# A written-out timetable of five engines is replaced by another one

## What is computed

```python
x = x + _L0_attn_a_ref(_layernorm(x, axis=-1), Wq, Wk, Wv, Wo)      # 16 heads of 8; causal, window of 32 plus every 64th key
x = x + _L0_ffn_ref(_layernorm(x, axis=-1), k0, k1, k2, s0, s1, s2)  # weights of +1 and -1, 256 -> 512 -> 512 -> 128
x = x + _L0_attn_b_ref(_layernorm(x, axis=-1), ln_g, ln_b, W_in, conv_w, ..., res_scale)   # a selective state space block
x = x + _L0_ffn_ref(_layernorm(x, axis=-1), k0, k1, k2, s0, s1, s2)
```

## Time and profile before

| what | before |
|---|---|
| median of 3 runs | 831.79 us (829.81 to 833.49) |
| span of the profiled execution | 829.0 us |
| lowest run | 829.81 us |
| instructions | 21435 |
| busy: TensorE, VectorE, GpSimd, ScalarE | 94%, 84%, 80%, 72% |
| mean granted TensorE clock | 0.994 |
| moved by DMA | 154.86 MB, 187 GB/s over the span |

### The profile page before, as it was taken

The page is one execution under the profiler, slowest core; times in us unless marked ns, Lnnn a source line. Parts: engine busy times, 40 slices in busy tenths (PEclk is TensorE's granted clock), DMA queues, the critical chain, the costliest instruction groups (busy, mean ns, idle before and its releaser), DMA issues. The chain is left out here.

```text
span 829.0 us, 21435 instructions
## 1 busy us (share of the span) xinstructions
PE 782.0 (94%) x7444; PEld 495.8 (60%) x7444; DVE 698.2 (84%) x1187; ACT 598.4 (72%) x1161; POOL 665.0 (80%) x824
## 2 busy tenths in 40 slices
PE   6999999999999999999999989998999999899997
PEld 5777647655665546556665457445565556456576
DVE  7775415999999988999599989999998998779992
ACT  5576498879769988896679978887658754765523
POOL 5116137998999989989898889989999999999771
PEclk9999999999999999999999999999999999999999
DMA  5000007997997849775398979789678989799950
GB/s 194 2 2 3 1 2 190 268 234 206 270 239 191 194 132 280 179 183 153 110 288 220 248 193 298 182 221 264 197 210 216 277 247 245 204 229 260 279 147 14
DMA packets 84174, 154.86 MB, mean 187 GB/s; under 512 B 9433, under 2 KB 10082, under 8 KB 84066
## 3 DMA queue, kind: packets, MB, share of 16 engines
q1 hardware_dynamic: 84066, 153.48, 70.6%
HBM read 142.43 MB, written 11.01 MB: 185 GB/s over the span
## 5 line engine op out<-in xcount | busy, mean ns | idle before, releaser
L1732 POOL TENSOR_TENSOR d<-d,cr 128x1024 f32<-128x1024 f32 x128 | 300.7, 2357 | 20.4 <-DVE d L1233 10.6
L1531 ACT ACTIVATE ps<-dt,An 128x512 f32<-128x512 f32 x256 | 175.2, 691 | 72.4 <-DVE d L1233 71.1
L1233 DVE TENSOR_TENSOR_SCAN d<-ps,hl,d 128x512 f32<-128x512 f32 x128 | 157.1, 1264 | 2.4 <-POOL d L1719 1.4
L1233 DVE TENSOR_TENSOR_SCAN d<-ps,d 128x512 f32<-128x512 f32 x128 | 150.4, 1205 | 7.0 <-POOL d L1719 5.7
L1221 DVE TENSOR_TENSOR d<-ps,d 128x512 f32<-128x512 f32 x184 | 119.3, 672 | 2.4 <-DMA d<-dud 2.3
L846 PE MATMUL ps<-h,w 128*128 128x512 f16 (+1 forms) x512 | 114.8, 373 | 2.5 <-DVE h L1178 1.6
L766 PE MATMUL ps<-KD,qm 128*128 128x128 f32 (+1 forms) x512 | 105.0, 339 | 2.0 <-DVE qm L1084 2.0
L968 PEld LDWEIGHTS ps<-cst 128*128 128x128 f32 x676 | 85.1, 197 | 26.2 <-issue 11.3
L968 PE MATMUL ps<-cst 128*128 128x128 f32 x676 | 90.5, 283 | 7.9 <-DMA cst<-in_w 4.4
L1719 POOL TENSOR_TENSOR d<-d,br 128x512 f32<-128x512 f32 x72 | 91.9, 1282 | 5.2 <-DMA d<-dud 5.2
L766 PEld LDWEIGHTS ps<-KD,qm 128*128 128x128 f32 x512 | 84.2, 197 | 14.7 <-DVE qm L1084 3.0
(11 more groups left out here) (178 smaller groups left out, 1397.1 us busy)
## 6 DMA issues: line engine op xcount, KB each, us to landing
dt<-dtd SPq DMA_DIRECT2D x256, 256.0 KB, 5.7
d<-dud SPq DMA_DIRECT2D x256, 256.0 KB, 5.5
dtd<-sR SPq DMA_DIRECT2D x16, 256.0 KB, 4.8
dud<-sE SPq DMA_DIRECT2D x16, 256.0 KB, 4.6
X<-in_x SPq DMA_DIRECT2D x8, 256.0 KB, 6.2
br<-bcd SPq DMA_DIRECT2D x8, 256.0 KB
cr<-bcd SPq DMA_DIRECT2D x8, 256.0 KB
out<-X SPq DMA_DIRECT2D x3, 512.0 KB, 6.2
```

What stands on the lines that cost most here:

```text
L1233: eng.tensor_tensor_scan(d, banks[u % NG][:, :], d, hl[:, r:r + 1] if m % 2 else 0.0, ALU.mult, ALU.add).then_inc(v_sc, 1)
L1531: eng.activation(banks[u % NG][:, :], DT[:, u % NT, :], ACT.Exp, scale=An[:, g:g + 1]).then_inc(s_da, 1)
L1732: eng.tensor_tensor(d, d, CR[m % 2][:, :].unsqueeze(1).to_broadcast((128, n, 512)), ALU.mult).then_inc(p_cm, n)
```

## The change

Every list in `PLACES` gets new numbers, and `WARM` gets a new, shorter list. Nothing else in the kernel differs: the steps, their instructions, their waits, the buffers and the indices are as before. Three kinds of steps and `WARM` stand for the whole table:

```diff
-    "vz_p": [2840],
+    "vz_p": [9297],
...
-    "drive_p": [141303, 142553, 147720, 159439, 174059, 176083, 179963, 191946, 206883, 217264, 221100, 228131, 234639, 246712, 254627, 274939,
+    "drive_p": [129795, 131029, 137621, 144009, 162317, 163551, 167765, 180513, 187455, 204685, 205919, 212804, 224857, 238033, 239267,
...
-    "scan_v": [142623, 146198, 149470, 152398, 153577, 154755, 155934, 159578, 160756, 161934, 163113, 164291, 171208, 175877, 177056, 179587,
+    "scan_v": [131260, 133583, 138298, 139427, 140556, 141685, 145560, 146689, 148777, 149906, 151035, 152164, 157021, 163921, 165050,
...
 WARM = [
-    (10117, 2, 20), (14676, 2, 5), (23177, 2, 3), (126618, 2, 3), (128753, 2, 4), (133485, 2, 2), (135682, 2, 1), (137887, 2, 1),
...
+    (185852, 7, 2), (206215, 7, 12), (236144, 6, 3), (470911, 7, 4), (558219, 5, 4), (576156, 4, 2), (606629, 6, 3), (632662, 6, 4),
```

More of the change, by code:

```diff
@@ new lines @@
+    "aback_v": [48220, 49937, 61525, 93723, 175992, 184432, 219875, 232383, 340818, 360095, 366020, 385443, 511030, 533136, 535582,
+        591485],
+    "afar_v": [25381, 25926, 29264, 36094, 36452, 43170, 47396, 47754, 120421, 127391, 127749, 145202, 148419, 160056, 171889, 172247,
+        274224, 274582, 288426, 288784, 306789, 318892, 335815, 336173, 446536, 462330, 462688, 463647, 480819, 499842, 509120, 509478],
+    "akd_v": [11844, 14659],
+    "akp_p": [14688, 171576, 348356, 474876],
@@ new lines @@
+    "aln_p": [4583, 6644, 49967, 52646, 132263, 134942, 320088, 327921],
+    "aln_s": [9207, 10038, 64637, 65131, 226995, 240707, 400291, 402236],
+    "aln_t": [8067, 9404, 62638, 63074, 226279, 239134, 398155, 398591],
+    "aln_v": [32112, 43528, 79876, 94392, 161608, 197749],
+    "an_s": [53202],
+    "ano_s": [6361, 8422, 57797, 58576, 211130, 234916, 360069, 360848],
+    "aown_s": [24571, 25600, 25998, 35768, 36091, 40682, 47070, 47242, 51317, 51427, 52715, 53092, 60601, 60711, 61341, 61718, 73134,
[5 rows of a table added]
@@ new lines @@
+    "jexp_s": [50217, 57651, 83387, 104288, 183004, 208541, 226225, 260124, 343271, 369964, 380333, 389373, 516576, 536967, 582663,
+        612298],
+    "jmix_p": [58674, 63240, 99062, 117769, 196772, 214038, 240501, 264805, 354738, 377445, 381883, 391785, 525841, 546882, 596402,
+        615326],
+    "jout_t": [64996, 66640, 110656, 121972, 200557, 222107, 252303, 271809, 378199, 381103, 386607, 402669, 547114, 550228, 619405,
+        623381],
+    "jrec_v": [58262, 62828, 98650, 113144, 195231, 210798, 237195, 264393, 353749, 373403, 381471, 391373, 523405, 546215, 593330,
+        614471],
@@ new lines @@
+    "lg_v": [760632, 760974],
+    "lm_t": [761117, 761563],
+    "lm_v": [761760, 762943],
+    "lmo_t": [756938, 757831],
+    "lpre_p": [722198],
+    "mln_p": [91347, 156785, 255958, 306934, 426193, 485341, 576052, 652198],
+    "mln_s": [95603, 161458, 261370, 313228, 430180, 488833, 580039, 655690],
+    "mln_t": [95262, 161142, 260276, 311547, 430108, 489325, 579967, 656113],
+    "mln_v": [90065, 154548, 253371, 304991, 424671, 482306, 573634, 650243],
+    "mno_s": [94103, 159683, 259339, 310242, 428900, 488048, 578759, 654905],
@@ new lines @@
+    "mout_t": [227092, 303167, 405360, 475450, 578102, 652303, 711089],
+    "mout_v": [231724, 306130, 407546, 477902, 580785, 654284, 713397],
+    "mu_s": [104434, 105017, 172625, 173318, 269324, 271347, 322803, 334282, 438831, 440880, 498320, 500578, 588685, 590248, 661243,
+        666867],
+    "mu_t": [97443, 100878, 165593, 169028, 264143, 267578, 317847, 330560, 433754, 437189, 493451, 496886, 583181, 586616, 657611,
+        661046],
+    "mx_d": [111898, 185654, 276299, 342941, 447091, 511295, 595261, 671614],
@@ L413 @@
+    "set_v": [20704, 77840],
+    "silu_s": [106699, 174525, 272274, 336096, 442894, 504121, 590970, 667589],
+    "store_d": [404468, 634482, 749805, 764110, 779105, 780962],
+    "vz_p": [9297],
+    "yev_v": [179164, 217085, 254510, 291670, 340163, 378301, 429805, 471897, 512296, 556746, 595510, 628186, 667295, 707980, 743345],
 }
 WARM = [
[9 rows of a table removed]
[4 rows of a table added]
 ]
```

153 lines of the change are left out of this document (63 added, 90 removed), and 321 rows, old and new, of tables (PLACES, WARM).

## The result

The change made the kernel 0.6% faster, not 3.6%: **826.43 us** (median of 18 runs, 820.88 to 832.55) against 831.38 (18 runs, 828.33 to 835.20) of the kernel before, a ratio of 0.9939 with an interval of 0.9918 to 0.9959. The forecast was 801.2 with a range of 791 to 816. It was wrong, by 25 us.

A forecast was written before the change was run, and what follows sets the result against it. GpSimd and VectorE, busy about 606 of 657.9 us across the scans, were taken as the bound. 829.0 - 9.3 - 21.3 = 798.4 us of span, plus 2.8 to the median, gave 801.2 us, range 791 to 816.

The forecast's parts named there:

- B: 144.4 to 802.3 us, all 256 scans: forecast 635.4 us, a gain of 21.3, between 13.2 and 26.4.
- A: 0 to 144.4 us, attention, first FFN pass and preparation of first scans: a gain of 9.3 us, between 2 and 11.3.
- C: Last 27 us, one chain from the last scan to the last addition: a gain of 0.
- cold start: Before the first scan: without start warm-ups, first transposes and products may meet 1.2 GHz, costing 2.0 us.
- drift: Between first and last scan: the 4.6 us the old order ran over its table, added to the new table's 625.7.
- reserve: Among the scans: tighter step spacing lets lateness show; GpSimd's 5.1 us taken, VectorE's 13.2 as the far bound.
- rival 2: Loads come late as DMA engines fill; load waits double or treble, 7.5 to 15 us back: 812 us, chance 0.14.
- Rival 3: Idle among the scans is only moved; they keep 657 us, only the start's gain counts: 822.5 us, chance 0.06.
- Rival 4: GpSimd and VectorE block each other more; all sixteen L1205 at 1.56 us add 14.9: 816 us, chance 0.04.
- Rival 5: TensorE's clock falls, mainly in the second half; over 20 falls on the path, 70 us low: 838 us, chance 0.04.
- Rival 6: The change does not do what it says; waits cancel elsewhere what it wins: 830 us, chance 0.04.
- The hole between scan 95 and scan 96: Largest single piece of the gain among the scans: 26.6 us by the old table, 19.4 by the new.

The follow-up runs named there:

- Identity: Kernel after with both Silu of each half replaced by Identity: 819.34 us; also with dt loads cut, 808.80, and with two more du buffers besides, 806.49.
- small loads: Kernel after with dt loads from u = 6 on cut to 32 of 128 partitions (64 of 256 KB): 813.46 us.
- 14 buffers: Kernel after with 14 instead of 12 du buffers, gate factor in 16 bit: 819.00 us; with the dt loads cut too, 810.26.
- the mixed order: Order of the kernel after up to the first scan, order of the kernel before from there on, 12 du buffers: 825.16 us.

## Why the prediction was wrong

- **The miss of 25.2 us** is B, 26.6 us longer than forecast, and A, 1.6 short of its gain, less 1.3 won in C and 1.7 because the span lies only 1.1 us under the median and not 2.8.
- **Stage A, 9.3 us: near.** 7.7 were won. The cold start was put at 2.0 and costs 0.9 to 1.1; the half's first table load, which the prediction had not seen, costs 2.1 (first scan at 134.6 with Identity; 133.9 and 134.2 in the other two kernels with it).
- **Stage B, 21.3 us: wrong; it lost 5.3.** The step that failed is the one sentence "I use the new intervals as what the new order needs if nothing comes late, and price from rows what comes late", with its prices 4.6 (drift) and 5.1 (reserve): 9.7 us, and at most 17.8 in its far bound, where 36.3 came. By the runs these are some 14.5 for loads, 3.8 for the halves' table loads when loads are relieved (8.4 when not), and 18.0 for the rest. The 3.8 is the least sure: by medians, less what the first scan gains, Identity brings B 5.0 us in after, 2.6 with small loads and 1.1 with 14 buffers as well, and the loads' part is then 16 to 17.
  - *Drift taken over from the old order, 4.6.* The table before contains idle itself: 652.1 us for 608 of work. The new one leaves 625.7 for the same work, so lateness of the same size no longer finds as much idle to fall into. That this is why the term grew is argued and not shown. Shown is its size: even with every cause found removed it is 18.0, four times the term.
  - *Reserve, 5.1.* Only the pitches of VectorE's and GpSimd's steps were compared. A kind that was really short was on ScalarE: `silu_s` at 3.316 for 4.61. It was there to be read in the table and the trace before.
  - *Loads.* They had no term in the sum, only rival 2. Nothing in the sum looked at how long before its use a load is placed. Lead against landing would have told it: by the table the lead is less than the landing time that the trace shows in 52 loads (27 dt, 25 du), by 38.7 us in sum; before it was 30 loads and 20.3 us. With the landing times of the trace before, which were at hand, load by load, the new table has 94 loads too short, by 100.2 us.
- **Rival 2 (loads come late, 0.14)** named the largest cause that a run has shown and a fair price for it: 7.5 to 15 us, measured 13 to 16. Its reason was off. It looked at the fill of the DMA engines; that did not move (0.86 in both, cut alike) and transfers landed as fast as before. What was short is buffers and lead against that landing time. Waits for loads grew sixfold, not two or three times.
- **Rival 3 (idle is only moved, 822.5, 0.06)** has the result nearest to the time measured, and that is 4 us above it, since B did not keep its 657. With 12 buffers the mixed order bears it out: the time is the same by either order of B. It is not true in general, since with 14 buffers the new order is 5.3 us faster.
- **Rival 4 (L1205 blocked):** its successor L1223 has a median of 0.46 us, below the 0.63 of before. It fell.
- **Rival 5 (clock):** seven falls instead of three, 27.2 us and not the 70 it asked for. VectorE was idle in some of them, against the forecast's 0 us each; 2.7 us of B by the estimate above, not isolated. **Rival 6:** the order did what it says up to the first scan.
- Right were the 606 us of GpSimd (603.7), the 256 warm-up pieces, and the sign. Stage C was put at 0 and gave 1.3. TensorE's busy time fell by 42, not 55: the warm-ups did take 56 off (90.5 to 34.5), but the other products took 14 more; 17 us more in falls of the clock can account for 8.5 at most. The hole between scan 95 and scan 96 shrank from 26.3 us to 23.6 (389.8 to 413.4), not to the table's 19.4.

The far bound of B was made from reserves alone, and the range ended at rival 2's 816. A bound in which all of VectorE's 49.5 us of idle stays would have ended at rival 3's 822.5, still 4 us too low.

What stays open: the 18.0 us that are left when loads, buffers and halves are relieved. The waits of VectorE and GpSimd there are many and short, none over 6.7 us in total for one line, and four falls of the clock lie among them; no run took one away alone.

## What to carry to other kernels

A schedule's table is a forecast of its own, and idle that it removes may be the reserve that kept it true: before trusting a tighter one, compare for every load the lead with the slow end of its landing times, and for every ring of buffers the round with buffers times pitch. Check each kind's spacing against the whole stretch in the trace, table loads and all. If a tighter order brings nothing, give it buffers: two more were worth 7.4 us to the new order and nothing to the old one. And before reading a stage's length from one profile, see where that execution lies among the others.

## What was not expected

Warm-up products put into planned gaps of TensorE cost 41.5 us, though 85 us of extra work was to lie in idle time: TensorE also stands some 25 us ahead of them, mostly for their banks, with products behind that others wait for. And moving loads forward, 2.2 us in the mean and each to a place where its buffer is free by plan, cost 16 us, as SyncE then stood at them (149 us instead of 96) and the other ring's loads came late: the waits for du went from 24.2 to 55.8 us.
